# Attention sums on a Trainium2 core: pair sums of the probabilities added a second time by an accumulating DMA

## The reference, cut to what matters

```
q = (query @ Wq).reshape(b, sq, 32, 32).transpose(0, 2, 1, 3)
k, v = the same with 8 key heads, each repeated 4 times      # 1024 keys
scores = einsum('bhqd,bhkd->bhqk', q, k) * 32 ** -0.5
probs = softmax(scores, axis=-1)
out = einsum('bhqk,bhkd->bhqd', probs, v)
...
return out @ Wo
```

## Time and profile before

| | |
|---|---|
| three runs, median | 1386.14 us (1383.67 to 1386.9) |
| profiled execution, its own time | 1389.39 us |
| span in its trace | 1387.6 us |
| TensorE busy | 1289.6 us, 93% of the span |
| VectorE busy | 840.5 us, 61% |
| GpSimd busy | 648.2 us, 47% |
| ScalarE busy | 446.8 us, 32% |

### The profile page before, as it was taken

One profiled execution on the slowest core, in us unless ns is written; L12 is line 12 of the kernel. 1 busy time (PEld: TensorE's weight loads), 2 busy tenths in 40 slices (PEclk: granted clock), 3 DMA queues, 4 the chain that ended last, 5 costly groups with the idle time before them and its releaser, 6 DMA issues.

```text
span 1387.6 us, 18180 instructions
## 1 busy us (share of the span) xinstructions
PE 1289.6 (93%) x6986; PEld 555.8 (40%) x6986; DVE 840.5 (61%) x1450; ACT 446.8 (32%) x804; POOL 648.2 (47%) x272
## 2 busy tenths in 40 slices
PE   5798778999998879999999999999979999999998
PEld 3455545444443322222222322224534444444443
DVE  7983991143344447888888888824466954363622
ACT  3683011101110026666666666671212101010000
POOL 5005615350003336778778877883014653453510
PEclk9989787999999989999999999999999999999999
DMA  8382213020004210010000001000023442452401
GB/s 311 115 304 72 80 47 91 31 61 0 0 25 138 75 58 18 19 36 18 19 27 27 18 18 35 1 1 1 0 81 122 140 144 91 148 164 67 137 0 60
DMA packets 38621, 97.17 MB, mean 70 GB/s; under 512 B 6160, under 2 KB 16400, under 8 KB 38544
## 3 DMA queue, kind: packets, MB, share of 16 engines
q1 hardware_dynamic: 37392, 91.94, 20.8%
q10 hardware_dynamic: 1152, 4.19, 0.7%
HBM read 85.49 MB, written 10.49 MB: 69 GB/s over the span
## 4 chain that ended last, share of the span: by engine, by line
PE 78%; DVE 15%; issue 2%; POOL 2%; ACT 2%; DMA 1%; SPq 0%; ACTq 0%; POOLq 0%; DVEq 0%
PE bank L559 46%; PE bank L767 12%; PE bank L754 8%; PE bank L806 6%; DVE mxp L1346 3%; PE bank L574 2%; PE bank L578 2%; PE bank L634 1%; DVE xn L1187 1%; DVE R L1152 1%; POOL R L535 1%; DVE XTl L1246 1%; DVE xn L1336 1%; DVE lnv L1184 1%; DVE R L1493 1%
## 5 line engine op out<-in xcount | busy, mean ns | idle before, releaser
L1346 DVE TENSOR_REDUCE mxp<-bank 128x1 f32<-128x512 f32 x512 | 317.4, 679 | 62.2 <-PE bank L754 61.5
L535 POOL TENSOR_TENSOR R<-R 128x2048 f32<-128x2048 f32 x64 | 290.2, 4535 | 80.2 <-ACT R L1073 80.2
L1073 ACT ACTIVATE R<-bank 128x512 f32<-128x512 f32 x512 | 271.7, 603 | 147.3 <-PE bank L806 145.2
L559 PE MATMUL bank<-XTh,R 128*128 128x512 bf16 x896 | 274.1, 383 | 10.0 <-POOL R L547 8.3
L480 POOL TENSOR_TENSOR R<-stage_w,zero 128x1024 f32 x36 | 70.1, 1946 | 358.2 <-DMA stage_w<-wts_in 230.2
L559 PE MATMUL bank<-R 128*128 128x512 bf16 x960 | 209.3, 379 | 2.3 <-DVE R L1528 2.0
L559 PE MATMUL bank<-XTl,R 128*128 128x512 bf16 x448 | 171.8, 383 | 0.0
L547 POOL TENSOR_TENSOR R<-stage_w,R 128x1024 bf16<-128x1024 f32 x32 | 76.1, 2392 | 172.2 <-DVE R L1493 172.2
L754 PE MATMUL bank<-R 96*128 96x512 bf16 x352 | 131.7, 385 | 15.0 <-DVE mxp L1346 11.0
L767 PE MATMUL bank<-R,stage_c 128*32 128x512 f32 x1024 | 137.5, 609 | 5.9 <-POOL stage_c L511 5.7
L559 PEld LDWEIGHTS bank<-R 128*128 128x128 bf16 (+1 forms) x960 | 93.8, 98 | 116.0 <-DVE R L1528 2.5
(11 more groups left out here) (174 smaller groups left out, 1467.0 us busy)
## 6 DMA issues: line engine op xcount, KB each, us to landing
stage_w<-wts_in SPq DMA_DIRECT2D x36, 512.0 KB, 3.6
stage_w<-w_in SPq DMA_DIRECT2D x32, 512.0 KB, 3.5
stage_c<-w_in SPq DMA_DIRECT2D x32, 512.0 KB, 3.5
R<-q_scr SPq DMA_DIRECT2D x48, 128.0 KB, 2.4
XTh<-ctx_nat_in SPq DMA_DIRECT2D x11, 512.0 KB, 4.7
XTh<-ctx_t_in SPq DMA_DIRECT2D x9, 512.0 KB, 5.2
X<-x_in SPq DMA_DIRECT2D x8, 512.0 KB, 7.1
q_scr<-R SPq DMA_DIRECT2D x32, 128.0 KB, 1.8
```

The source lines that it names most:

```text
L535: pool.tensor_tensor(PS[j % 2], PB[2 * j % 4], PB[2 * j % 4 + 1], ALU.add).then_inc(p_add, 1)
L559: mm = pe.matmul(o, a, m, start=first and a is ah and bs is bh, stop=last and a is al)
L1073: act.activation(PB[kt % 4][:, h * S:(h + 1) * S], bank[t_bank(g, t)][:, :], ACT.Exp, scale=float(HD) ** -0.5).then_inc(exp_done, 1)
L1346: dve.tensor_reduce(mxp[head // REP % 2][:, m, n // 2, n % 2:n % 2 + 1], bank[s_bank(u)][:, :], AX.X, ALU.max).then_inc(s_max, 1)
```

## The change

GpSimd still makes four adds a group. Pair sums 0 and 2 are written to buffers `PS[0]` and `PS[2]`, pair sums 1 and 3 both to `PS[1]`; behind each of the latter GpSimd issues a DMA that adds the 1 MB of `PS[1]` onto `PS[0]` or `PS[2]` inside SBUF. TensorE then does two summing quadruples a group instead of four, at t = 10 and 26 of the next group. `PS[2]` is the two `stage_w` buffers made into one. GpSimd waits before add 3 for the first DMA of the group, before add 1 for the second DMA of the group before, and before adds 0 and 2 for the quadruples that read their buffers. `sums_out` moves from t = 12 to t = 28, `invert` goes a group later to t = 2, 6, 10, 14, and `divide(g - 2)` stands behind the DMA issue of j = 1. Behind the last group, the last quadruple stands behind output tile 1.

```diff
+TOTAL_AT = (10, 26)
+SUM_OUT_AT = 28
...
-        stage_w = [sb(f"stage_w{i}", [P, D], F32) for i in range(2)]
+        stage_pair = sb("stage_pair", [P, 2 * D], F32)
+        stage_w = [stage_pair[:, i * D:(i + 1) * D] for i in range(2)]
...
-        PS = [R[4]... for i in range(2)]
+        PS = [R[4]... for i in range(2)] + [stage_pair[:, :]]
...
                     pool.wait_ge(exp_done, STEPS * g + 2 * REP * (j + 1))
-                    if 4 * g + j >= 2:
-                        pool.wait_ge(one_mm, 4 * g + j - 1)
-                    pool.tensor_tensor(PS[j % 2], PB[2 * j % 4], PB[2 * j % 4 + 1], ALU.add).then_inc(p_add, 1)
+                    if j == 3:
+                        pool.wait_ge(ps_sum[0], 16 * (g + 1))
+                    elif g > 0 and j == 1:
+                        pool.wait_ge(ps_sum[1], 16 * g)
+                    elif g > 0:
+                        pool.wait_ge(one_mm, 2 * (g - 1) + j // 2 + 1)
+                    pool.tensor_tensor(PS[(0, 1, 2, 1)[j]], PB[2 * j % 4], PB[2 * j % 4 + 1], ALU.add).then_inc(p_add, 1)
+                    if j % 2 == 1:
+                        pool.wait_ge(p_add, 4 * g + j + 1)
+                        pool.dma_start(PS[j - 1], PS[1], accum_op=ALU.add).then_inc(ps_sum[j // 2], 16)
                     if j == 0 and 1 <= g < GROUPS - 1:
                         stage_values(g + 1)
-                    if g > 0 and j == (1 if g == GROUPS - 1 else KT // 2 - 1):
-                        divide(g - 1)
+                    if g >= 2 and j == 1:
+                        divide(g - 2)
+            divide(GROUPS - 2)
             divide(GROUPS - 1)
...
             def total(g, j):
-                pe.wait_ge(p_add, 4 * g + j + 1)
+                pe.wait_ge(ps_sum[j], 16 * (g + 1))
                 if j == 0 and g > 0:
                     pe.wait_ge(sum_out, g)
-                over_keys(bank[6], onesf[:, 0:HD], PS[j % 2], j == 0, j == KT // 2 - 1).then_inc(one_mm, 1)
+                over_keys(bank[6], onesf[:, 0:HD], PS[2 * j], j == 0, j == 1).then_inc(one_mm, 1)
...
-                    if t % 8 == 2:
-                        if t > 10:
-                            total(g, t // 8 - 2)
-                        elif g > 0:
-                            total(g - 1, KT // 2 - 2 + t // 8)
+                    if g > 0 and t in TOTAL_AT:
+                        total(g - 1, TOTAL_AT.index(t))
...
             output_tile(0)
-            total(GROUPS - 1, KT // 2 - 2)
             weigh(GROUPS - 1, KT - 1)
-            total(GROUPS - 1, KT // 2 - 1)
+            total(GROUPS - 1, 0)
             output_tile(1)
+            total(GROUPS - 1, 1)
...
-                    if g > 0 and t == 12:
+                    if g > 0 and t == SUM_OUT_AT:
                         sums_out(g - 1)
...
-                    if g > 0 and t >= STEPS // 2 and t % 4 == 2:
-                        invert(g - 1, t // 4 - 4)
+                    if g > 1 and t < STEPS // 2 and t % 4 == 2:
+                        invert(g - 2, t // 4)
+            for quarter in range(4):
+                invert(GROUPS - 2, quarter)
```

More of the change, by code:

```diff
@@ L195, in build @@
         VS = [stage_c[1][:, S + i * KT * HD:S + (i + 1) * KT * HD] for i in range(2)]
-        PS = [R[4][:, :].bitcast(F32)[:, i * REP * S:(i + 1) * REP * S] for i in range(2)]
+        PS = [R[4][:, :].bitcast(F32)[:, i * REP * S:(i + 1) * REP * S] for i in range(2)] + [stage_pair[:, :]]
         o_raw = [stage_c[0][:, i * S:(i + 1) * S] for i in range(2)]
@@ L282, in build @@
         p_add = sem("p_add")
+        ps_sum = [sem(f"ps_sum{i}") for i in range(2)]
         one_mm = sem("one_mm")
@@ L1060, in sums_out @@
             def sums_out(g):
-                act.wait_ge(one_mm, 4 * (g + 1))
+                act.wait_ge(one_mm, 2 * (g + 1))
                 if g > 0:
```

## The result

| | before | after |
|---|---|---|
| median (runs) | 1386.52 us (4) | 1406.80 us (4: 1402.47 to 1411.61) |
| ratio, 95% interval | | **1.0146 [1.0101, 1.0190]** |
| profiled execution, span | 1389.39, 1387.6 us | 1409.11, 1407.3 us |
| TensorE / GpSimd busy | 1289.6 / 648.2 us | 1282.2 / 677.1 us |

The change makes the kernel 1.5% slower, 20 us. The forecast was 1381 us, the range 1374 to 1406.

What follows compares the result with a forecast made beforehand. TensorE was taken to set the pace (26.78 of 26.88 us a group), VectorE and GpSimd close behind. Savings of 1.7 + 1.7 + 7.9 less 6.5 at the end gave 4.8: 1386.14 - 4.8 = 1381 us, range 1374 to 1406.

Steps and rivals of the forecast that it cites:

- The transfer L: Landing time of the 1 MB behind its issue, before adds 3 and 1: 5.8 to 6.5 us, hidden below 7.0.
- the 0.09 DMA share: DMA busy for 0.09 of the steady stretch before the change, cited against the transfer deciding the pace.
- The end: Behind output tile 1, last quadruple, copy and reciprocals delay `turn(0)`: 6.5 us lost on TensorE.
- GpSimd's path: From exp t = 7 to the next group's, through adds, issue, `divide` and waiting exp: 26.2 us a group.
- 25.2 + i: Length in us of GpSimd's path per group, with i the DMA issue on GpSimd, taken as 1.0.
- groups 2 to 13: Steady groups fall from 26.88 to 26.2 us each: 8.2 us saved, put at 7.9.
- Groups 14 and 15: Last two groups, fewer or no score tiles, GpSimd already setting the pace: 0 saved.
- path of 26.2 us: Steady group's time by GpSimd's path with an issue of 1.0 us, so 0.7 saved instead of 1.7.
- A: Adds 3 and 1 wait for the DMA, landing 7.0 us or more: slower, 1396 to 1424; chance 0.28.
- B: DMA issue on GpSimd takes 2 us, a group 27.2: 8 us slower, 1394; chance 0.14.
- D: Issue under 0.6 us, TensorE and VectorE hold groups at 25.8: 10 us saved, 1376; chance 0.05.
- signs of being wrong: Adds 1 and 3 released by DMA, issue 1.5 us or more, attention clock below 1.00, no gap before `turn(0)`.

Runs made afterwards that it cites:

- e1: Changed kernel with the transpose of the row maxima and the two 4 KB row transfers four steps earlier (t = 20 and 22): 1394.77 us, ratio 1.0064.
- e7: Kernel before plus two 1 MB accumulating transfers a group onto a buffer nobody reads, order and quadruples as before: 1400.28 us, ratio 1.0102.
- e4: Changed kernel with the last group's third and fourth pair sums given their own quadruples ahead of output tile 1, no last transfer: 1398.67 us, ratio 1.0073.
- e10: e1 with `divide` over 128 of 512 columns for all groups but the last, the other outputs left out: 1383.62 us, ratio 0.9985.
- e3: Changed kernel with accumulating transfers of 64 KB instead of 1 MB, other columns left out, 1 added to each row sum: 1390.76 us, ratio 1.0029.
- e8: e1 with `divide(g - 1)` behind the DMA issue of j = 3 and its reciprocals at t = 29, 31, 2 and 6: 1400.63 us, ratio 1.0122.
- e12: e11 with the last group's third and fourth pair sums given their own quadruples, no last transfer: 1379.52 us, ratio 0.9958.
- e11: e1 with `stage_values` and `divide(g - 2)` both behind add 2, and the second quadruple at t = 22 instead of 26: 1390.58 us, ratio 1.0035.

## Why the prediction was wrong

**The step that failed: the transfer was weighed only against its own waits.** "The transfer L" asked when the 1 MB is there for adds 3 and 1, and had that nearly right: 5.8 to 6.5 us forecast behind the issue, 7.0 to 7.2 measured from the issue's start, of which 0.87 is the issue; adds 1 and 3 hardly ever wait for it. Not asked was whom the transfer holds up on the 16 engines. The prediction even took the 0.09 DMA share as comfort; with the change it is 0.47. The two small transfers at t = 26, with some 2.3 us to spare until t = 0 (they land 3.6 us later now, and in most groups TensorE waits 1.1 to 1.4 us), were in the kernel's text and in no term of the sum. Issued four steps earlier they land in 1.7 us, and the kernel takes 12.0 us less (e1; the interval of the changed kernel's own ratio is 6 us to either side). About half of it is the low clock behind the waits. This is an estimate: the four groups at low clock are together 13.0 us longer than the same groups of e1, and their waits are together 6 us longer than four of the usual 1.2 us. The transfers alone in the old order cost 14 us (e7). This is the largest term, but not the only error: without it (e1) the change is still 8 us slower than the kernel before. What made the 1 MB transfer itself take up to 9.2 us instead of 7.0 in some groups stays open.

**The end: mechanism right, size off.** Forecast 6.5 us lost, measured 8.1 by e4 and 10.4 in the trace. The wait was 7.4 us, at the upper edge of the 6.0 to 7.5 forecast, and the low clock behind it, which the prediction counted on nowhere, makes up the rest.

**The groups: mechanism right, the gain too large.** GpSimd's path through add 1, issue, divide, add 2 and the exp that waits does set the pace (e10). It was worked out as 25.2 + i; with the issue at 0.87 and the wait ahead of it at 0.30 instead of 0.07 that is 26.3, measured 26.46. Counted on TensorE, from the first weighing quadruple of one group to that of the next, e1 against the kernel before (us):

| groups | before | e1 | saved | forecast |
|---|---|---|---|---|
| 0 and 1 | 55.3 | 51.6 | 3.7 | 3.4 |
| 2 to 13 | 322.6 | 320.4 | 2.1 | 7.9 |
| 14 | 24.9 | 26.4 | -1.5 | 0 |
| 15, up to output tile 0 | 18.2 | 19.9 | -1.7 | 0 |
| all | 421.0 | 418.4 | 2.7 | 11.3 |

Groups 0 and 1 came out as forecast. In groups 2 to 13 a usual group saves 0.42 instead of 0.66, and a few longer ones, most of them absent in e3, take 3 us of that back. Groups 14 and 15 were put at nothing because GpSimd already set the pace there. But the prediction's own path of 26.2 us is longer than the 25.58 that group 14 took by another mark, so a loss was to be expected: with the change group 14 takes as long as a steady group, though it has fewer score tiles. With `divide` moved out from between adds 1 and 2, group 14 takes 25.2 us (e8) and 25.1 (e12). Group 15 was not tried by itself.

**The sum again.** In the two profiled executions the groups save 2.7 (e1), the rows cost 14.6 (433.0 us in the changed kernel against 418.4 in e1, first weighing quadruple to output tile 0), and the end costs 10.4: together 22.3. The spans differ by only 19.7, since work that the change does not touch took 6.0 us less ahead of attention and 3.3 more behind `turn(1)`. By medians the rows are 12.0 and the end 8.1, together 20.1 of the 20.3 between the kernels, with nothing left for the groups. The 2 to 3 us between the two ways of counting are within the spread of the runs.

**The rivals.** A (the transfer decides through adds 1 and 3) was wrong for the usual group of this kernel, e3 shows it, and costs some 4 us in a few others (e1 against e3); it comes true once the order around it is better (e11). B (a dear issue) was wrong: 0.87 us. D's floor of 25.8 is close to the 25.88 of e10, but what holds that run was not shown. None of the cases had the rows. A granted clock below 1.00 stood among the signs of being wrong, and it came, but no case had a price for it. The upper end of the range, 1406, was drawn from A and fell 0.8 us short.

## What to carry to other kernels

A large transfer put into a stage has two prices: when it lands, and what every small transfer that is issued while it runs has to wait; list the small ones of the stage with the step that waits for each, and issue them ahead of the large one. A long wait on TensorE can cost more than its length: here 3.1 us of waiting were followed by 5.4 us at half clock, 2.5 us more. And of work taken off the leading engine (1.7 us a group) only as much comes back as separates it from the next engine's path, here 0.4 us. The order of that engine's list then brought 4.6 us in attention (e11 against e1 in the profiles), more than the 2.7 us of the quadruples.

## What the runs showed of the hardware

- A 4 KB transfer issued 2.0 to 2.5 us behind a 1 MB accumulating one lands in 5.2 us instead of 1.7, in the worst case 7.0; behind a copy of the same size in 2.5. It comes in at about the time that the large one ends: in the worst case the large one releases add 3 at 750.62 and the small one the matmul at 750.87. How the engines share their time was not measured any further.
- An accumulating transfer of 1 MB inside SBUF takes 7.0 us (up to 9.2), a copy 4.6 to 4.7, an accumulating one of 64 KB 2.4.
- The issue of an accumulating transfer on GpSimd lasts 0.87 us, that of a copy 0.57, with 0.30 us of waiting before it. The next instruction starts 0.6 us behind the start of the issue; behind an accumulating one its first 1.3 us become 1.6.
- In the changed kernel TensorE ran at 1.2 GHz after waits of 3.13, 2.79, 2.68 and 2.40 us, 5.4 us long after the first, and at full clock after eleven waits of 1.09 to 1.42 us. The length of the wait alone does not decide: after one of 2.50 us in e4 the next 4.8 us had a granted clock of 1.00, and soon after one of 1.87 us in e7 the clock was 0.51 for 3.5 us.
